# Four fused cross-attention layers on one core: the mask rows of the first two batches get a turn, a copy and a transfer of their own, and two loads go from SyncE's queue to ScalarE's

## The reference

```python
# L0: 16 heads of 8 features, masked, then layer norm
q, k, v = x @ wq, ctx @ wk, ctx @ wv
s = einsum("bqhd,bkhd->bhqk", q, k) / sqrt(8)
s = s * m - (1 - m) * 1e10
x = layer_norm(softmax(s) @ v @ wo + bo + x)
# L1: 16 heads of 64 features over ctx
x = x + softmax(rms_norm(x) @ wq1 @ (ctx @ wk1).T) @ (ctx @ wv1) @ wo1
# L2: routed self-attention, cross-attention, feed-forward
# L3: cross-attention over ctx, then layer norm
```

## Time and profile before

| | |
|---|---|
| median of three runs | 343.07 us (342.51 to 345.08) |
| the profiled execution, its time | 343.29 us |
| its span, first to last instruction | 341.4 us |
| outside the span | 1.9 us |
| TensorE busy | 293.8 us, 86% of the span |
| VectorE, ScalarE, GpSimd busy | 236.7, 212.9, 92.7 us |

### The profile page before, as it was taken

One profiled execution on the slowest core, in us unless ns is written; L12 is line 12 of the kernel. 1 busy time (PEld: TensorE's weight loads), 2 busy tenths in 40 slices (PEclk: granted clock), 3 DMA queues, 4 the chain that ended last, 5 costly groups with the idle time before them and its releaser, 6 DMA issues.

```text
span 341.4 us, 10348 instructions
## 1 busy us (share of the span) xinstructions
PE 293.8 (86%) x4157; PEld 220.2 (64%) x4157; DVE 236.7 (69%) x480; ACT 212.9 (62%) x463; POOL 92.7 (27%) x261
## 2 busy tenths in 40 slices
PE   7889999988989989988988899889869986996871
PEld 4535657766868768866766676666547764784650
DVE  6566498259886666767766578787886657775855
ACT  4377778666677776876755666457655544555550
POOL 3025353110310000001413734514433304314131
PEclk9999999999999999999999999999998999999896
DMA  6879900000000000001320324312330011011001
GB/s 198 233 182 243 356 6 2 2 2 0 2 2 2 2 0 2 2 0 42 84 64 25 85 80 134 104 49 78 110 93 3 8 44 48 4 46 49 17 18 31
DMA packets 26735, 20.93 MB, mean 61 GB/s; under 512 B 3256, under 2 KB 25664, under 8 KB 26432
## 3 DMA queue, kind: packets, MB, share of 16 engines
q1 hardware_dynamic: 23360, 18.24, 19.0%
q10 hardware_dynamic: 3328, 2.04, 2.1%
HBM read 6.11 MB, written 0.52 MB: 19 GB/s over the span
## 4 chain that ended last, share of the span: by engine, by line
PE 48%; ACT 15%; DVE 12%; issue 7%; POOL 5%; SPq 5%; DMA 4%; ACTq 2%; POOLq 0%
PE psum L364 7%; ACT probs L867 5%; PE psum L825 4%; SPq L692 4%; DMA qs<-part_q 4%; PE psum L791 4%; PE psum L766 4%; PE psum L740 3%; ACT probs L875 3%; PE psum L322 3%; PE psum L337 3%; PE psum L592 3%; PE psum L986 2%; PE psum L802 2%; PE psum L817 2%
## 5 line engine op out<-in xcount | busy, mean ns | idle before, releaser
L489 DVE TENSOR_REDUCE maxs<-psum 128x8 f32<-128x1024 f32 x64 | 77.5, 1213 | 37.4 <-PE psum L337 28.6
L415 ACT ACTIVATE probs<-psum 128x1024 f32<-128x1024 f32 x64 | 65.6, 1025 | 34.6 <-PE psum L330 21.8
L364 PE MATMUL psum<-probs,vpad 128*32 128x128 f32 x1024 | 35.4, 280 | 0.0
L867 ACT ACTIVATE probs<-psum,maxs 128x128 f32<-128x128 f32 x128 | 34.8, 390 | 0.5 <-DVE maxs L916 0.5
L364 PEld LDWEIGHTS psum<-probs,vpad 128*32 128x32 f32 x1024 | 26.6, 111 | 12.0 <-issue 6.9
L337 PE MATMUL psum<-ks,qs 64*128 64x128 bf16 x512 | 25.7, 221 | 9.9 <-DMA qs<-part_q 3.3
L322 PE MATMUL psum<-qs,ks 64*128 64x128 bf16 x512 | 25.7, 221 | 8.4 <-ACT probs L415 8.2
L550 POOL TENSOR_SCALAR rstd<-stats 128x2 f32<-128x2 f32 (+1 forms) x19 | 4.2, 223 | 99.8 <-DVE stats L516 99.7
L322 PEld LDWEIGHTS psum<-qs,ks 64*128 64x128 bf16 x512 | 14.6, 95 | 21.8 <-ACT probs L415 10.8
L926 DVE TENSOR_REDUCE mres<-probs 128x8 f32<-128x1024 f32 x16 | 19.5, 1218 | 12.6 <-ACT probs L867 12.6
L916 DVE TENSOR_REDUCE maxs<-psum 128x8 f32<-128x1024 f32 x16 | 19.5, 1220 | 11.7 <-PE psum L791 11.7
(11 more groups left out here) (159 smaller groups left out, 627.8 us busy)
## 6 DMA issues: line engine op xcount, KB each, us to landing
qs<-part_q SPq DMA_DIRECT2D x63, 64.0 KB, 2.0
ks<-part_k SPq DMA_DIRECT2D x30, 128.0 KB, 2.4
ks<-part_k SPq DMA_DIRECT2D x36, 64.0 KB, 2.0
wmat<-in_wmat SPq DMA_DIRECT2D x1, 1856.0 KB, 10.5
qs<-part_q ACTq DMA_DIRECT2D x21, 64.0 KB, 2.2
wmat<-in_wmat SPq DMA_DIRECT2D x1, 1024.0 KB, 7.0
qs<-part_q SPq DMA_DIRECT2D x6, 128.0 KB, 5.2
wrow<-in_wrow SPq DMA_DIRECT2D x1, 704.0 KB, 8.6
```

What stands on the lines that cost most here:

```text
L364: mm = e.matmul(o_bank(n)[rg(c), bt(half)], vpad[:, n % 2, 4 * half + c, G * a:G * a + G], pt, start=(a == 0), stop=(a == 1), skip_group_c ...
L415: e.activation(probs_of(n, half), bank(4, 2), ACT.Exp, scale=layer(n).scale)\
L489: e.tensor_reduce(maxs[:, n % 2, 8 * half:8 * half + 8], bank(2 * half, 2).rearrange("p (h k) -> p h k", k=P), AX.X, ALU.max, negate=True)\
L867: ins = e.activation(probs[:, half, bt(s)], bank(2 * half, 2)[:, bt(s)], ACT.Exp, bias=maxs[:, b % 2, 8 * half + s:8 * half + s + 1])
```

## The change

The mask rows are handled in two pieces. The first two batches of `up` are turned into bank 7, ahead of the broadcast of the mask of batches 2 and 3. They are copied by themselves and sent by themselves, and S of batch 0 waits for this piece. The six others are turned into bank 3 after the projections of batches 2 and 3. They are copied and sent next, under the semaphore `slots2`, which S of batch 2 now awaits with 64 in place of 48. The loads of `x` and `wrow` leave SyncE's order. ScalarE issues them in step 1, behind its two copies L674 and ahead of the copies of L1 values 1 and 2. Line numbers shift by 2 to 6 behind the edits.

```diff
             if n == 2:
-                ready += [(sem("slots2"), 48)]
+                ready += [(sem("slots2"), 64)]
@@ sync
             e.wait_ge(sem("kaug_out"), 1)
-            e.dma_start(ks0[ROW_SLOT::8, :, :], kaug[:, :]).then_inc(sem("kaug_in"), 16)
+            e.dma_start(ks0[ROW_SLOT::8, :, 0:PAIR], kaug[:, 0:PAIR]).then_inc(sem("kaug_in"), 16)
+            e.wait_ge(sem("kaug_out"), 2)
+            e.dma_start(ks0[ROW_SLOT::8, :, PAIR:T], kaug[:, PAIR:T]).then_inc(sem("slots2"), 16)
             fill_slots(e, 2, 6)
...
-            e.dma_start(x[:, :, :], x_d).then_inc(sem("in_x"), 16)
-            e.dma_start(wrow[:, :], wrow_d.partition_broadcast(P)).then_inc(sem("in_rows"), 16)
@@ tensor
-            pe_mask_rows(e, 2, 2, 6)
             e.wait_ge(sem("identB"), 1)
             e.wait_ge(sem("up"), 3)
-            kb = bank(3).bitcast(BF16)
-            for b in range(B):
-                mm = e.transpose(kb[:, bt(b)], up[:, b, :], identB[:, :])
+            for b in range(2):
+                mm = e.transpose(bank(7).bitcast(BF16)[:, bt(b)], up[:, b, :], identB[:, :])
             mm.then_inc(sem("kaug_mm"), 1)
+            pe_mask_rows(e, 2, 2, 6)
...
             pe_proj(e, L0, "q", 2, 2, 5)
+            for b in range(2, B):
+                mm = e.transpose(bank(3).bitcast(BF16)[:, bt(b)], up[:, b, :], identB[:, :])
+            mm.then_inc(sem("kaug_mm"), 1)
             e.wait_ge(sem("in_v0"), 16)
             pe_v(e, L0, 0, 2)
-            e.wait_ge(sem("kaug_out"), 1)
+            e.wait_ge(sem("kaug_out"), 2)
@@ scalar
                     act_p1(e, L0, "q", 4, 4)
                     act_p1(e, L0, "k", 4, 4)
+                    e.dma_start(x[:, :, :], x_d).then_inc(sem("in_x"), 16)
+                    e.dma_start(wrow[:, :], wrow_d.partition_broadcast(P)).then_inc(sem("in_rows"), 16)
@@ vector
             e.wait_ge(sem("kaug_mm"), 1)
-            e.tensor_copy(kaug[:, :], bank(3).bitcast(BF16)).then_inc(sem("kaug_out"), 1)
+            e.tensor_copy(kaug[:, 0:PAIR], bank(7).bitcast(BF16)[:, 0:PAIR]).then_inc(sem("kaug_out"), 1)
             dve_raw(e, 2, 2, 4)
+            e.wait_ge(sem("kaug_mm"), 2)
+            e.tensor_copy(kaug[:, PAIR:T], bank(3).bitcast(BF16)[:, PAIR:T]).then_inc(sem("kaug_out"), 1)
```

More of the change, by code:

```diff
@@ L1083, in extra0 @@
                     e.wait_ge(sem("slots0"), 48)
-                    e.wait_ge(sem("slots2"), 48)
+                    e.wait_ge(sem("slots2"), 64)
                     for g in range(2):
```

## The result

| | before | changed |
|---|---|---|
| median of 20 runs each | 343.01 us (339.25 to 346.34) | 345.32 us (343.75 to 350.68) |
| ratio, with its 95% interval | | 1.0088 (1.0064 to 1.0112) |
| the profiled execution, its time and span | 343.29 and 341.4 us | 349.48 and 347.6 us |

The changed kernel is slower by 2.3 us by the medians, and by 3.0 us by the ratio. That is inside 1%, but it is 1.6 us above the forecast and 0.1 us above the end of the range. The profiled execution is one of the long ones, which the ratio leaves out; so the kernel was profiled twice more without any edit, and executions of 344.38 and 345.62 us were caught. Each of the two is the second shortest of its series (12 and 7 executions). How often each comes in the executions that were not profiled is not known.

The account below looks back on a forecast made before the run. PE, busy 86%, bounds the kernel, but SP's issue pace sets S of batch 2 at 23.93. From 343.29 us, +0.7 there and -0.1 at batch 4 give 343.9, or 343.7 on the median; range 342.2 to 345.2.

Parts of the forecast that it names:

- The sum: Whole kernel: S of batch 2 +0.7 us, gap at S of batch 4 -0.1, rest 0; +0.6 on the median.
- a lead of 0.5 us: PE at the first L740: what stays of the 1.19 us won at S of batch 0; ends 0.3 and 1.19.
- Part 1, first half: S of batch 0: first mask piece lands at 12.7, so the 1.19 us wait goes and S starts near 12.9.
- Part 1, second half: First L740: L1 value weights land 5.0 us after issue, at 17.92, leaving 0.3 us of lead; 0.5 taken.
- Part 2: SP's queue: one more issue, 0.64 us; last q slot of batch 3 issued at 20.97, landing at 23.7.
- Part 3: ACT, step 1: issues of x and wrow take 2.0 us, delay the copies; S of batch 2 0.7 us late.
- rival A: ACT's two issues take only 0.68 us, S of batch 2 up to 0.8 us earlier; 342.6 us, chance 0.22.
- rival B: GpSimd: wrow lands at 34 to 35, delaying the split of batch 3; 345.4 to 346.4 us, chance 0.08.
- Part 4: Batches 4 to 7: slots issued 1.4 us earlier, no gap at S of batch 4 (-0.1 us); wrow at 31, free.
- The two rivals on the late side: ACT's issues both meeting long packets (2.84 us), 344.8 us, chance 0.10; and rival B, chance 0.08.

Follow-up runs that it names:

- mask_fills_first: `mask_only` with SP's second piece of mask rows behind the fills of slots 6 and 7; 343.17 us, ratio 1.0026.
- mask_only: Changed kernel with x and wrow back in SP's order, so only the mask rows in two pieces; 343.75 us, ratio 1.0021.
- mask_filler: `mask_only` with eight unused turns on PE ahead of the wait for the L1 value weights; 341.35 us, ratio 0.9960.
- loads_only: Kernel before with only the loads of x and wrow moved to ACT, mask rows as before; 342.54 us, ratio 0.9968.
- x_only: Changed kernel with wrow back in SP's order, so only x is on ACT; 346.00 us, ratio 1.0098.
- changed_filler: Changed kernel with eight unused turns on PE ahead of the wait for the L1 value weights; 346.42 us, ratio 1.0110.
- behind_v1: Changed kernel with x and wrow issued on ACT behind the copies of L1 values 1 and 2; 342.99 us, ratio 0.9997.

## Why the prediction was off

**The direction was right, by luck.** The sum had +0.7 us from ACT's issues and took a lead of 0.5 us from the mask rows. In the three profiles of the changed kernel the issues cost nothing and the lead was lost, and the loss came from what the sum did not have. That a shift of S of batch 2 goes to the end nearly in full is shown as far as 220 us. The two shorter executions have shifts of 2.4 and 2.6 us there, and are 1.1 and 2.3 us longer in all than the profiled one of the kernel before.

**Part 1, first half: right.** S of batch 0 was forecast at 12.9, and started at 12.69, 12.68 and 12.95 in the three executions (and as late as 14.01 in other kernels of the study). PE's new wait ahead of L740 was there as forecast. With S so early, its second half once waited for a copy of ScalarE's (L712) by 0.35 us.

**Part 1, second half: the step that failed.** "They are issued by ACT at 12.92 ... and landed 5.0 us later, at 17.92. If that stays, ... 0.3 us of the lead is left." It did not stay. The landings came 6.4 and 6.6 us after the issue in the two shorter executions and 5.3 us in the long one, at 19.05, 19.06 and 18.1. The lead of 0.3 to 1.19 us was a loss of 0.84 us in these two, and only 0.1 us of it was left in the long one. Issuing these weights 0.3 or 0.5 us earlier gained nothing. That SP's transfers beside them fill the engines until then is likely and not shown; `mask_fills_first` tests a part of it. The landings of `mask_only` (5.8 us after 13.84) and `mask_filler` (6.3 us after 12.31) fall between 18.6 and 19.7 too.

**What was missing from the sum.** PE's wait moved from S of batch 0 (1.19 us) to L740 (1.79 and 1.99 us), and there the clock fell to half for 6.8 us, at 2.34 us of lost time. I had counted a wait only by its length. No term and no rival had the clock, although it is the largest single item of the two shorter executions. Over all executions the changed kernel has about 5 us more half clock. At 0.34 us lost for each (2.34 over 6.8), that is 1.7 us, an estimate, or some half of the loss. It cannot be added to the overtaking, since the waits that this makes are followed by half clock too.

**Part 2.** "The last slot of q is issued at 20.97 in place of 20.33." It was at 21.61, 22.38 and 21.86. The extra issue was rightly 0.6 us. The rest are long issues in front of it (in the 349.48 us execution 2.13 us for two, where they take 1.24). It landed at 25.6, 26.6 and 29.7 in place of 23.7.

**Part 3: the second step that failed.** "ACT reaches the two DMAs when its second L674 starts, ... and everything behind them waits until they are issued." They took 0.33 + 0.46, 0.33 + 0.56 and 0.33 + 0.73 us instead of 2.0, close to rival A's 0.68. They ran beside the exponential, before L674. They held up no copy. The 0.7 us that I put there is not in these traces; it is in that of `loads_only`, where the issues took 2.01 us, ACT stood 0.95 us ahead of the copies, and S of batch 2 came at 24.55. The true cost lay where I saw none. With x issued 0.5 to 1.8 us ahead of it, the last slot landed after 4.2 us (`x_only`), 5.9, 6.7 and 7.8 us, in place of 2.0 to 3.55.

The Trainium skill (page "DMA: Bandwidth & Descriptors", section "Queues, rings and completion order") has the engines go round between queues packet by packet, and a packet be drained whole before the switch, with 9 to 17 descriptors as typical. I had read this in rival B as turns in small pieces, and as a mild cost to wrow. The traces rule out turns row by row (203 against 8 from 21.2 to 24 us). In `changed_filler` the turns were whole loads, x and then wrow. The 128 rows of x are 8 for each of the 16 engines if they are spread evenly, so a whole load would be no more than one such packet; that is an estimate from the page's figure, and no run here tests it. Turns of this size, in which the queue that came second stands still for a load, would have been a rival with a price of 1 to 6 us. The evidence was in the trace of the kernel before, where SP's queue stood at 0.5% beside the weights. I had looked only at how fast the weights landed.

**Part 4.** wrow landed early enough in each profiled execution of the changed kernel. Its residual started at 32.34 in the 344.38 us execution, without a wait, and the split of batch 3 ended 1.4 us ahead of its turn (37.25 against 38.64). The gap at S of batch 4 was gone as forecast, at 38.32, 0.22 us behind its L330. In `loads_only`, where PE is early and the slots are not, the landing binds by 0.94 us, as that part had warned for such a kernel.

**The range.** The two rivals on the late side were priced one by one (344.8, 345.4 to 346.4). The late landing and the clock behind it are one chain: in the two shorter executions a wait of 1.8 to 2.0 us came with 2.3 us more. That chain alone gives a shift of +2.4 us, which no case had.

## What to carry to other kernels

Where two queues feed one waiting instruction, compare the times of issue, not the orders in each program. A load of 512 KB on the second queue, issued less than two microseconds ahead of a small urgent transfer on the first, held it up by 1 to 6 us here. Issued 0.03 to 1.1 us behind it, it still left it 4.0 us in place of 2.0 to 3.55; 2 us behind, it cost nothing. Place such a load behind something that comes surely later than the urgent issue. And when an early wait is taken from TensorE, ask where the idle time goes: gathered in one place ahead of a late transfer, it came with half clock in two of the three profiles of the changed kernel and cost about twice its length. Last, one profile of a kernel whose order is a race between two queues shows one outcome. Here the first profile showed a loss of 6 us of a kind that the next two did not have.

## What was not expected of the hardware

- DMA issues on ScalarE start while computing work that stands ahead of them in its program is still to begin (20.05 against 20.77 and 21.27 us). Copies behind a long issue do wait for it (`loads_only`: wrow's issue ends at 23.29, the copies start at 23.33).
- A large transfer on one queue can all but stop another queue: 0.8% against 92.9% of the 16 engines for 2.8 us, 0 packets against 62 for 1.5 us in `changed_filler`, and 6.4 us to land in place of 3.2 for `kaug`.
- TensorE's clock fell to half within a wait of 1.8 to 2.0 us in the middle of a busy stretch, for 6.8 us, and within the wait of 6.77 us for 10.2 us. With eight turns in front of a shorter wait (0.85 us in `mask_filler`) it stayed full. A wait of 1.18 us did not lower it in `mask_only`, and one of 0.62 us did in `behind_v1` (two L740 at 2.08 us), so the length of the wait alone does not tell.
